# First transfers in another order: edge rounds ahead of W1, W2 and x, small transfers on ScalarE's queue

## The reference

```python
h = jnp.maximum(_layernorm(x, axis=-1), 0.0)
agg = jax.ops.segment_sum(edge_attr, receivers, num_segments=N_NODES)   # 106250 rows -> 6250
y = jnp.concatenate([agg, h], axis=1)                                   # 6250 x 256
return x + (jax.nn.relu(y @ W1 + b1) @ W2 + b2)                         # 256 -> 512 -> 128
```

## Time and profile before

| | us |
|---|---|
| median of 3 runs | 219.62 (219.38 to 221.08) |
| the profiled execution | 219.51 |
| its span | 217.4 |
| busy: PE | 191.9 (88%) |
| busy: DVE | 132.7 (61%) |
| busy: ACT | 83.7 (38%) |
| busy: POOL | 43.5 (20%) |

### The profile page before, as it was taken

The page is one execution under the profiler, slowest core; times in us unless marked ns, Lnnn a source line. Parts: engine busy times, 40 slices in busy tenths (PEclk is TensorE's granted clock), DMA queues, the critical chain, the costliest instruction groups (busy, mean ns, idle before and its releaser), DMA issues.

```text
span 217.4 us, 6713 instructions
## 1 busy us (share of the span) xinstructions
PE 191.9 (88%) x2525; PEld 163.3 (75%) x2525; DVE 132.7 (61%) x579; ACT 83.7 (38%) x181; POOL 43.5 (20%) x120
## 2 busy tenths in 40 slices
PE   1326979989889999999999999999999999999970
PEld 0214868769669889889798898898988988978860
DVE  2532777797887767747747567477575684751110
ACT  3131045253253361383343623823535238234300
POOL 4464112220220222112202211122022112200000
PEclk9999999999999999999999999999999999999997
DMA  6999999999999998999989999999999970100101
GB/s 216 302 372 372 376 374 376 376 377 377 384 376 311 368 351 280 370 348 310 379 292 384 374 316 377 322 309 362 311 383 375 292 265 7 51 0 3 48 3 39
DMA packets 44590, 62.54 MB, mean 288 GB/s; under 512 B 1763, under 2 KB 44262, under 8 KB 44556
## 3 DMA queue, kind: packets, MB, share of 16 engines
q1 hardware_dynamic: 43150, 60.78, 80.6%
q10 hardware_dynamic: 1406, 1.30, 1.8%
HBM read 58.88 MB, written 3.20 MB: 286 GB/s over the span
## 4 chain that ended last, share of the span: by engine, by line
PE 69%; DVE 11%; DMA 7%; issue 3%; ACT 2%; SPq 1%; DVEq 1%; POOL 1%; ACTq 0%; POOLq 0%
PE bank L754 19%; PE bank L698 17%; PE bank L733 13%; PE bank L742 13%; DMA edges<-in_edge_attr 7%; DVE onehot L430 3%; PE bank L709 3%; DVE aggT L512 2%; PE bank L719 2%; ACT agg_hi L359 1%; DVE agg_lo L470 1%; ACT hidden L369 1%; DVE halves L443 1%; DVEq L496 1%; PE bank L691 1%
## 5 line engine op out<-in xcount | busy, mean ns | idle before, releaser
L698 PE MATMUL bank<-edges,onehot 128*32 128x128 f32 x1656 | 54.2, 285 | 6.6 <-DMA edges<-in_edge_attr 6.1
L698 PEld LDWEIGHTS bank<-edges,onehot 128*32 128x32 f32 x1656 | 46.0, 114 | 14.5 <-DMA edges<-in_edge_attr 7.8
L754 PE MATMUL bank<-w,hidden 128*128 128x128 f32 (+1 forms) x400 | 48.2, 278 | 0.7 <-ACT hidden L369 0.7
L754 PEld LDWEIGHTS bank<-w,hidden 128*128 128x128 f32 (+1 forms) x400 | 45.5, 189 | 3.5 <-issue 3.4
L369 ACT ACTIVATE hidden<-bank,b_col 128x512 f32<-128x512 f32 (+2 forms) x52 | 33.8, 663 | 36.6 <-PE bank L742 36.5
L338 ACT ACTIVATE xn<-xs,shift,rstd 128x128 f32<-128x128 f32 (+1 forms) x50 | 21.8, 484 | 62.8 <-POOL shift L302 62.8
L512 DVE TENSOR_TENSOR aggT<-bank,aggT 128x32 f32 x277 | 35.5, 189 | 15.9 <-issue 9.1
L295 POOL TENSOR_SCALAR var<-meanvar 128x2 f32<-128x2 f32 (+1 forms) x25 | 7.3, 293 | 138.6 <-DVE meanvar L448 138.6
L430 DVE TENSOR_TENSOR onehot<-relT,iota 128x384 f32<-128x384 f32 x69 | 34.3, 551 | 0.4 <-ACT iota L373 0.4
L464 DVE TENSOR_TENSOR hT_lo<-bank,hT_hi 128x256 fp32r<-128x256 f32 (+1 forms) x25 | 10.4, 415 | 19.0 <-ACT hT_hi L345 19.0
L733 PE MATMUL bank<-hT_hi,w_hi 128*128 128x512 f32 (+2 forms) x52 | 21.2, 408 | 0.0
(11 more groups left out here) (91 smaller groups left out, 166.9 us busy)
## 6 DMA issues: line engine op xcount, KB each, us to landing
edges<-in_edge_attr SPq DMA_DIRECT2D x69, 768.0 KB, 8.5
out_rows<-outrow SPq DMA_DIRECT2D x11, 256.0 KB
xs<-in_x SPq DMA_DIRECT2D x21, 128.0 KB, 8.6
w<-in_L_gnn_W ACTq DMA_DIRECT2D x1, 512.0 KB, 7.4
xs<-in_x ACTq DMA_DIRECT2D x1, 384.0 KB, 3.6
hidden<-in_dst SPq DMA_DIRECT2D x2, 192.0 KB, 5.6
w<-in_L_gnn_W ACTq DMA_DIRECT2D x1, 256.0 KB, 10.5
out_rows<-outrow SPq DMA_DIRECT2D x2, 128.0 KB
```

The source lines that it names most:

```text
L698: ins = nc.tensor.matmul(sums_ps[t * W:(t + 1) * W, cols], onehot[:, hots, e, :], edges[:, slot, e * F:(e + 1) * F], start=(g == 0), stop= ...
L754: ins = nc.tensor.matmul(out_ps[0:w, (2 * i + j) * F:(2 * i + j + 1) * F], hidden[:, t, at:at + w], w2[:, t, :], start=(t == 0), stop=(t = ...
```

## The change

The first transfers are issued in another order and partly from the other engine. SP now issues dstA, round 0, round 1, W1, round 2, x of blocks 1 and 2, rounds 3 and 4, W2, rounds 5 to 7, and x of the last block. ACT now issues x of block 0, dstB, dstC, dstD, b1 and b2. The transfer of x of blocks 0 to 2 is cut in two, with a semaphore of its own for blocks 1 and 2. All other instructions stay as they are.

```diff
         x_first_landed = sem("x_first_landed")
+        x_next_landed = sem("x_next_landed")
...
             load(0)
-            sp.dma_start(dstB[:, :], dst[P * CHUNK:2 * P * CHUNK].rearrange("(c e) -> c e", e=CHUNK)
-                         ).then_inc(dst_landed[1], 16)
-            sp.dma_start(dstC[:, :], dst[2 * P * CHUNK:FULL * CHUNK].rearrange("(c e) -> c e", e=CHUNK)
-                         ).then_inc(dst_landed[2], 16)
-            sp.dma_start(dstD[:, :], dst[FULL * CHUNK:E].rearrange("(a e) -> a e", a=1)).then_inc(dst_landed[3], 16)
-            for r in range(1, RING):
+            load(1)
+            sp.dma_start(w1[:, :, :], W1.rearrange("(t p) h -> p t h", p=P)).then_inc(w1_landed, 16)
+            load(2)
+            sp.dma_start(xs[:, 1:3, :], x_v[:, 1:3, :]).then_inc(x_next_landed, 16)
+            load(3)
+            load(4)
+            sp.dma_start(w2[:, :, :], W2.rearrange("(t p) f -> p t f", p=P)).then_inc(w2_landed, 16)
+            for r in range(5, RING):
                 load(r)
+            sp.dma_start(xs[0:NLAST // 2, NB - 1, :], x_last_v).then_inc(x_last_landed, 16)
...
         def _(act):
-            act.dma_start(xs[:, 0:3, :], x_v[:, 0:3, :]).then_inc(x_first_landed, 16)
-            act.dma_start(w1[:, :, :], W1.rearrange("(t p) h -> p t h", p=P)).then_inc(w1_landed, 16)
+            act.dma_start(xs[:, 0, :], x_v[:, 0, :]).then_inc(x_first_landed, 16)
+            act.dma_start(dstB[:, :], dst[P * CHUNK:2 * P * CHUNK].rearrange("(c e) -> c e", e=CHUNK)
+                          ).then_inc(dst_landed[1], 16)
+            act.dma_start(dstC[:, :], dst[2 * P * CHUNK:FULL * CHUNK].rearrange("(c e) -> c e", e=CHUNK)
+                          ).then_inc(dst_landed[2], 16)
+            act.dma_start(dstD[:, :], dst[FULL * CHUNK:E].rearrange("(a e) -> a e", a=1)).then_inc(dst_landed[3], 16)
             act.dma_start(b1_row[:, :], b1.rearrange("(t p) -> t p", p=P)).then_inc(b1_landed, 16)
             act.dma_start(b2_all[:, :], b2.partition_broadcast(P)).then_inc(b2_landed, 16)
-            act.dma_start(w2[:, :, :], W2.rearrange("(t p) f -> p t f", p=P)).then_inc(w2_landed, 16)
-            act.dma_start(xs[0:NLAST // 2, NB - 1, :], x_last_v).then_inc(x_last_landed, 16)
...
             def stats(b):
-                if b < 3:
+                if b == 0:
                     dve.wait_ge(x_first_landed, 16)
+                elif b < 3:
+                    dve.wait_ge(x_next_landed, 16)
```

## The result

The changed kernel takes 217.88 us (median of 20 runs, 217.03 to 220.09), the kernel before 219.48 (20 runs). The ratio is 0.992, with a 95% interval of 0.990 to 0.995: 1.6 us or 0.8% faster. In a later comparison on the chip it was 217.64 against 219.10, ratio 0.992 (0.988 to 0.996). Its profiled execution has a span of 216.0 us, 1.4 less than before.

The account below looks back on a forecast made before the run. Round 3's landing was taken to end last in the chain that sets the one-hots and PE's unbroken stretch. With x of blocks 1 and 2 then late, one-hots come 1.65 us earlier: 219.51 - 1.65 = 217.9 us, range 216.4 to 219.6.

Parts of the forecast that it names:

- Round 3: Landing of round 3's transfer, which PE waits for: from 19.4 to 17.1 us, by 0.7 and 1.6 us.
- the lone engine: Last block's x, 53 packets seemingly on one engine taking turns with the rounds: costs rounds 1 to 3 1.6 us.
- full price: One engine held for all 53 KB at 23 KB a us, 2.3 us; as a rival, gain 2.1, 217.4 us.
- x of blocks 1 and 2: Its landing, L, which DVE's statistics of block 1 wait for: 14.6 us, bounds 14.1 and 15.0.
- the dip: DMA at only 220 GB/s from 7 to 9.5 us, 1.04 us against 375; forecast to stay.
- What hangs on L: Fixed steps from block 1's statistics, 5.89 us, then 1.83 us: one-hots of rounds 4 to 6 at 22.4, 1.65 earlier.
- After 24 us: From round 8 on landings keep their times: round 12 at 38.9, block 4's x at 36.7; users come 1.65 us earlier.
- The cap on the gain: Block 4's x, landing at 36.7 before DVE wants it at 37.1, limits the gain to 2.1 us.
- The wait of PE for round 12: PE stands 1.0 us near 38, covered by its 1.24 us wait for DVE ahead of L709.
- The larger gain: Rival: dip goes, gain 2.7, 216.8 us; or one engine costs its full 2.3 us, 217.4. Together 27%.
- The slower case: Rival, 8%: SP's one queue supplies too little; gain gone at 270 GB/s from 5 us on, 221.9 us at 220.
- Given back: Rival, 20%: waits for landings from round 8 on take back the gain, 218.9 us, or 219.5 if more goes.

Follow-up runs that it names:

- Experiment 1: Kernel before, with only x of the last block issued by SP behind round 7 instead of by ACT: 218.34 us against 219.38, ratio 0.992.
- experiment 3: Kernel before, with only W2's transfer moved from ACT to SP, behind round 4: 218.82 us, ratio 0.994.
- experiment 2: Kernel before, with x of the last block cut into transfers of 48 and 5 partitions, in its old place on ACT's queue: 217.72 us, ratio 0.990.
- experiment 6: Changed kernel, with x of blocks 1 and 2 issued right behind round 0: 217.66 us, ratio to the kernel before 0.991.
- experiment 8: Changed kernel, with x of the last block issued at block 12's turn instead of behind round 7: 217.17 us against 217.64 for the changed kernel.
- experiment 11: The changed kernel itself, measured again: 217.64 us, ratio to the kernel before 0.992.
- experiment 7: Changed kernel, with b2 issued by SP behind round 4 instead of by ACT at the start: 218.15 us, ratio to the kernel before 0.994.
- experiment 10: The kernel of experiment 9, with b2 also issued by SP behind round 4: median 218.30 us, six times from 215.17 to 219.63.
- experiment 12: The kernel of experiment 10, with the first store also issued ahead of rounds 18 to 20: 216.14 us, ratio to the kernel before 0.984.
- experiment 9: Changed kernel; x of blocks 1 and 2 behind round 0, block 4's ahead of round 8, the last block's at block 12's turn: 217.45 us, ratio 0.990.

## Why the prediction was right

The time (217.9 forecast, 217.88 measured) and the mechanism were right, and the steps stand as follows.

*Round 3* was forecast at 17.1 and came at 16.88. The two terms were W2 with 0.7 and the lone engine with 1.6 us. Experiment 1 measures the second by itself as 1.65, experiment 3 the first by itself as 0.4. The Trainium skill's rule of one engine agrees with experiment 2 and with the two events of the transfer's semaphore. Of the 2.3 us that I worked out with it as a full price, the rounds lost 1.65 here; with W2 out of the way (experiment 3) the one engine was 2.46 us behind the others.

*x of blocks 1 and 2* was forecast to land at 14.6, and DVE used it at 14.76. That it, and not round 3, would set the one-hots is shown by experiment 6. The bytes counted for it were right by two errors that offset each other: the dip was deeper (154 GB/s for 207) and the stretch behind it faster (386 for 362). The 0.7 to 1.4 us added to that count were what the count left over in the kernel before, with no cause named; here 1.3 us lie between the count (13.4) and the landing (14.73), and what they consist of stays open.

*What hangs on L* was 5.9 us to the low part of h in both kernels (14.76 to 20.66). The rest, from the copy of the turned dstB on, was sized at 1.83 us and took 1.49. In the kernel before that piece seems to have held a second, unmarked wait of 0.2 to 0.3 us for PE's transposes of dstC and dstD (L525 starts 0.79 us behind L520 there, L533 0.56 behind L528 here). So the one-hots came at 22.06, not 22.4.

*After 24 us* is where a step failed. "From round 8 on every landing keeps its time" was wrong by 0.5 us: x of block 4 landed at 37.3 instead of 36.7 and round 12 at 39.4 instead of 38.9. The cap on the gain, forecast at 2.1, was therefore 1.5 us, and it was in force. The wait of PE for round 12 was 1.58 and not 1.0, and it was covered, as forecast: the statistics of block 4 are 1.48 us earlier than before and the stretch 1.49, so nothing was lost between them. Two small errors, 0.34 us too little at the one-hots and 0.5 too much behind them, made the sum of 1.65 look better than its parts (measured at the stretch: 1.49). The 0.5 us hang on the same transfer of 53 partitions, since experiment 8, which moves it alone, gives them back. In the kernel before it was through at 18.11, and by block 4's x the last of the 16 events came only 0.9 us behind the fifteenth (36.75 and 35.84). Here it was through at 28.40, and the gap was still 1.3 us (experiment 11: 37.27 and 35.94); in experiment 8 it is 0.2. The prediction counted the same bytes ahead of round 8 and left out that 53 KB of them go through one engine, now right ahead of these landings.

*The rivals.* The larger gain did not come since the dip stayed where it was; experiment 7 shows that b2's transfer, issued by ACT at the start as before, is the dip. The Trainium skill's rule on issuing engines ("DMA: Bandwidth & Descriptors", section "Issuing engines are not separate DMA queues"), by which the split over queues is worth nothing, fits with that, but no run here tests it: experiment 7 changes b2's engine and its place at once. The slower case had its point at 270 GB/s from 5 us on, and SP's queue almost alone carried 386 from 9 to 14. "Given back" was true for 0.5 us.

## What to carry to other kernels

Count the packets that a transfer puts on its busiest engine, not its bytes: one transfer of 54 KB over 53 partitions delayed the rounds queued beside it by 1.65 us, and cut into 48 and 5 partitions it did not. Only 53 was tried here. When a wait at the start is shortened, list the next landings that other engines need and their margins before adding up the gain; here they were x of block 4, then the first store, and each took its turn as the cap. The whole change gave 1.6 us; the five edits on top of it, most of which gave little or nothing by themselves, brought that to 3.0.

## What the runs showed of the hardware

A broadcast load of one row of 512 bytes to 128 partitions (64 KB written) held all of DMA at 154 GB/s for 2 us while ACT's queue carried it at the start. With that transfer behind round 4 on SP's queue the same 2 us ran at 378, and in the new place no like dip appeared (14 to 20 us at 344 to 355 GB/s in experiments 7, 10 and 12). Why it costs less there wasn't tried.

The granted clock falls for short pieces at places that differ between executions of like kernels. From 58 to 66 us it was 0.79 in experiments 1, 6, 9 and 10, and 1.00 in the changed kernel:

```profile
58.00:66.00 8.00, 6.87 (x77) 5.43 (x81) 5.66 (x27) 3.97 (x8) 1.47 (x4) 0.79 1.05 373
```

That is experiment 1, where the 12 products of L742 took 4.63 instead of 3.02 us. Ahead of the fall, from 30 to 58 us, PE was busy for 25.79 us there and for 25.52 in the changed kernel, which kept its clock. Such a fall fits the two groups of times in experiment 9, about 1.4 us apart: the mean clock is 0.993 and 0.994 in the lower three and 0.976 to 0.985 in the upper three. Ahead of 30 us a low clock can cost nothing: in experiment 8 it was 0.58 from 14 to 20 us and 0.74 from 20 to 30, and the stretch of PE still started 37.46 us behind the one-hots (37.47 in the kernel before); the median, 217.17, was the second lowest of all.
